# One GpSimd chain for both layer norms of a chunk, and a new order in the preparation of chunk 0, in a Mamba and MoE kernel

## The reference, cut to what matters

```python
# x is (8, 1024, 256); ED = 512 channels, N = 16 states, K = 4 taps
x = x + attn(_layernorm(x))        # a Mamba block
x = x + ffn(_layernorm(x))         # a shared expert and routed experts

# in attn:
xz = einsum('bld,ed->ble', x, in_proj_w); xp, z = halves of xz
xc = silu(causal depthwise conv of xp over 4 positions)
dBC = xc @ x_proj_w.T              # dt (64), Bm (16), Cm (16)
delta = softplus(dt @ dt_proj_w.T + dt_proj_b)
dA = exp(delta * A);  BX = delta * Bm * xc
hs = scan over positions of h = dA * h + BX      # per channel and state
y = sum over n of hs * Cm + D * xc
out = (y * silu(z)) @ out_proj_w.T

def _layernorm(x, eps=1e-05):
    m = mean(x); v = var(x)
    return (x - m) / sqrt(v + eps)
```

## Time and profile before

| | us |
|---|---|
| median of 3 runs (1570.89 to 1573.24) | 1572.64 |
| profiled execution, its own time | 1570.26 |
| its span in the trace | 1568.1 |
| mean granted TensorE clock | 0.993 |
| DVE busy | 1474.4 (94%), 1773 instructions |
| PE busy | 1448.2 (92%) |
| POOL busy | 1410.3 (90%), 1248 instructions |
| ACT busy | 1257.9 (80%) |
| DVE scans, L950 | 1165.5 (1024 of 1201 ns) |
| POOL products, L1238 | 1210.4 (512 of 2365 ns) |
| POOL u, L1256 | 81.7 (64 of 1276 ns) |
| POOL power, L1266 and L1277 | 16.2 and 15.1 (16 and 15 of about 1.01 us) |

### The profile page before, as it was taken

One profiled execution on the slowest core, in us unless ns is written; L12 is line 12 of the kernel. 1 busy time (PEld: TensorE's weight loads), 2 busy tenths in 40 slices (PEclk: granted clock), 3 DMA queues, 4 the chain that ended last, 5 costly groups with the idle time before them and its releaser, 6 DMA issues.

```text
span 1568.1 us, 39429 instructions
## 1 busy us (share of the span) xinstructions
PE 1448.2 (92%) x15188; PEld 1124.8 (72%) x15188; DVE 1474.4 (94%) x1773; ACT 1257.9 (80%) x2100; POOL 1410.3 (90%) x1248
## 2 busy tenths in 40 slices
PE   8889999999999999999999999999999999998887
PEld 5666777676776777777777776777777776776776
DVE  6999999999999999999999999999999999998885
ACT  7887887887888888887887888888887887787761
POOL 2899999999999999999999989999998999999993
PEclk9999999999999999999999999999999999999999
DMA  5103032040402204031040402204031030402201
GB/s 155 65 3 136 2 97 69 7 158 3 136 29 69 96 3 162 2 100 65 13 152 3 136 28 71 95 3 162 2 102 63 13 139 3 150 2 70 95 15 42
DMA packets 78514, 106.49 MB, mean 68 GB/s; under 512 B 42289, under 2 KB 67761, under 8 KB 70130
## 3 DMA queue, kind: packets, MB, share of 16 engines
q1 hardware_dynamic: 78322, 103.92, 20.7%
HBM read 86.10 MB, written 17.30 MB: 66 GB/s over the span
## 4 chain that ended last, share of the span: by engine, by line
DVE 31%; PE 20%; ACT 19%; issue 15%; POOL 10%; DMA 2%; SPq 1%; DVEq 1%; ACTq 0%; POOLq 0%
DVE hs L950 27%; PE BX L236 9%; ACT da L614 8%; POOL hs L1238 8%; PE Y L296 4%; PE Y L260 3%; DMA cb<-c_scratch 1%; ACT xc L681 1%; ACT x2n L751 1%; PE PB L346 1%; SPq L1367 1%; DVE st L962 1%; ACT xp L649 1%; ACT u L719 1%; DVE Y L981 1%
## 5 line engine op out<-in xcount | busy, mean ns | idle before, releaser
L1238 POOL TENSOR_TENSOR hs<-hs,cb 128x1024 f32<-128x1024 f32 x512 | 1210.4, 2365 | 67.2 <-DVE hs L950 45.2
L950 DVE TENSOR_TENSOR_SCAN hs<-da,BX 128x512 f32<-128x512 f32 x1024 | 1165.5, 1201 | 59.8 <-PE BX L236 50.5
L614 ACT ACTIVATE da<-delta,a_neg 128x511 f32<-128x511 f32 (+1 forms) x1024 | 663.6, 711 | 24.9 <-DVE hs L950 24.4
L260 PEld LDWEIGHTS Y<-ident,hs 128*128 128x128 f32 x4096 | 467.4, 141 | 92.9 <-issue 62.5
L260 PE MATMUL Y<-ident,hs 128*128 128x128 f32 x4096 | 514.0, 274 | 8.5 <-POOL hs L1238 8.5
L236 PE MATMUL BX<-bd,uT 32*128 32x128 f32 x8192 | 303.1, 285 | 96.6 <-DVE hs L950 91.4
L236 PEld LDWEIGHTS BX<-bd,uT 32*128 32x128 f32 x8192 | 253.7, 187 | 157.3 <-DVE hs L950 155.0
L296 PE MATMUL Y<-xnT,w_in 128*128 128x512 f32 x240 | 119.5, 621 | 0.9 <-ACT xnT L630 0.9
L649 ACT ACTIVATE xp<-Y 128x512 f32<-128x512 f32 x60 | 35.9, 598 | 101.2 <-PE Y L296 100.7
L321 PE MATMUL PA<-w_in,xnT 128*128 128x512 f32 x240 | 114.5, 599 | 0.0
L981 DVE SCALAR_TENSOR_TENSOR Y<-xp,w_conv,Y 128x512 f32<-128x512 f32 x120 | 88.9, 741 | 2.6 <-ACT Y L651 0.9
(11 more groups left out here) (186 smaller groups left out, 1496.9 us busy)
## 6 DMA issues: line engine op xcount, KB each, us to landing
cb<-c_scratch SPq DMA_DIRECT2D x64, 1024.0 KB, 4.8
x<-in_x SPq DMA_DIRECT2D x16, 512.0 KB, 4.0
x_scratch<-x2T SPq DMA_DIRECT2D x16, 512.0 KB, 6.6
...
c_scratch<-dbc SPq DMA_DIRECT2D x64, 8.0 KB, 1.5
```

The lines of the kernel that those rows point to most:

```text
L260: mm = e.matmul(Y[(G * c + g) % 2][:, t * P:(t + 1) * P], hs[:, k % HR, q, t * P:(t + 1) * P], ident[:, :], is_transpose=True, start=False ...
L614: e.activation(da[:, k % DR, q, h:], delta[:, g, h:], ACT.Exp, scale=a_neg[:, g, n:n + 1]).then_inc(s_da, 1)
L950: e.tensor_tensor_scan(hs[:, k % HR, q, :], da[:, k % DR, q, :], BX[:, :].rearrange("p (t n) -> p n t", n=RT)[:, n % RT, :], float(c % HV) ...
L1238: e.tensor_tensor(hs[:, k % HR, :, :], hs[:, k % HR, :, :], cb[:, Q * p:Q * p + Q, :], ALU.mult).then_inc(s_hc, 1)
```

## The change

1. Buffers `mv`, `ve`, `rstd`, `neg`, `shift` become 8 columns wide; the first norm has columns 0 to 3, the second 4 to 7. In chunks 1 to 12 (`BOTH`) POOL runs one chain over all 8 columns at step 21, where it ran one of 4 columns at step 21 and another of 4 at step 25. Chunk 0 has its one chain (of 4) at step 21 instead of 25; chunks 13 to 15 keep theirs. Who waited for the second norm's semaphore now waits for the joint one (`shifted2`).
2. In the preparation of chunk 0: the norm of chunk 1 moves on ACT from ahead of the first evacuations to behind the second SiLU. DVE evacuates `dbc` in place of ACT. DVE computes the first `u` in place of POOL. The z projections 3 and 2, their evacuations, the first `act_exp` (now in two parts) and the `act_skip` of group 0 are put in another order.
3. At step 3 of chunk 0, PE runs 8 matmuls of the identity into `PA` whose result nobody reads.

```diff
@@ tensor
             pe_dbc(e, 0, 1)
-            pe_z_first(e, 3, (0,))
             pe_dt(e, 0, 0)
             pe_bt(e, 0)
             pe_dt(e, 0, 1)
-            pe_z_first(e, 3, (1,))
-            pe_z_first(e, 2)
+            pe_z_first(e, 3)
             pe_ut(e, 0, 0)
+            pe_z_first(e, 2, (0,))
             e.wait_ge(s_d1_out, 1)
             pe_bx(e, 0)
             pe_trc(e, 1, 0)
             pe_trc(e, 1, 1)
+            pe_z_first(e, 2, (1,))
...
+                    if c == 0 and s == 3:
+                        e.wait_ge(s_pa_out, a_use["trc", 1, 1] + 1)
+                        for _ in range(8):
+                            e.matmul(PA[:, 0:P], ident[:, :], ident[:, :], start=True, stop=True)
@@ scalar
             act_trc(e, 0, 1)
-            act_norm(e, 1)
...
             act_silu_first(e, 1)
+            act_norm(e, 1)
             act_silu_first(e, 2)
             act_z_first(e, 0)
-            act_z_first(e, 1)
             act_silu_first(e, 3)
             e.preload_act_table_set(EXPS)
-            act_dbc(e, 0)
+            act_z_first(e, 1)
...
-            act_exp(e, 0)
+            act_exp(e, 0, (0,))
             act_ut(e, 0, 0)
+            act_exp(e, 0, (1,))
             act_z_first(e, 3)
-            act_z_first(e, 2)
             act_exp(e, 1)
             act_trc(e, 1, 0)
             act_trc(e, 1, 1)
-            act_skip(e, 0, 0)
+            act_z_first(e, 2)
             act_exp(e, 2)
@@ vector
             dve_aggr(e, 2)
+            e.wait_ge(s_pa, a_use["dbc", 0, 0] + 1)
+            e.tensor_copy(dbc[0:FX, :].rearrange("f (j q t) -> f q j t", j=J, q=RT),
+                          PA[0:FX, :].rearrange("f (q j t) -> f q j t", j=J, q=RT)).then_inc(s_pa_out, 1)
             dve_stats(e, 3, 0)
             dve_stats(e, 3, 1)
             dve_bd(e, 0)
             dve_delta(e, 0, 0)
+            e.wait_ge(s_pb_out, b_use["dt", 0, 0] + 1)
+            e.wait_ge(s_xc, 1)
+            e.tensor_tensor(u[:, 0, :].rearrange("p (j q t) -> p q j t", j=J, q=RT),
+                            delta[:, 0, :].rearrange("p (q j t) -> p q j t", j=J, q=RT),
+                            xc[:, 0, :].rearrange("p (q j t) -> p q j t", j=J, q=RT), ALU.mult).then_inc(s_u, 1)
@@ gpsimd
         def pool_rstd(e, c):
             e.wait_ge(s_mv, TB * (c + 1))
             e.wait_ge(s_xn, c)
+            n = TB
+            if BOTH[0] <= c - 3 <= BOTH[1]:
+                n = 2 * TB
+                e.wait_ge(s_mv2, TB * (c - 3))
+                e.wait_ge(s_xn2, c - 4)
+            e.tensor_tensor(ve_b[:, 0:n], mv_b[:, 0:n, 1], epsv[:, 0:n], ALU.add).then_inc(s_ve, 1)
...
-            pool_u(e, 0, 0)
+            e.wait_ge(s_u, 1)
             pool_u(e, 0, 1)
...
-                    if s == 21 and on(c - 1):
+                    if s == 21 and c > BOTH[1]:
                         pool_rstd2(e, c - 1)
...
-                    if s == 25 and on(c + 3):
+                    if s == 21 and on(c + 3):
                         pool_rstd(e, c + 3)
```

More of the change, by code:

```diff
@@ L98, in mamba_moe @@
         mask = sb("mask", [P, KT])
-        mhalf = sb("mhalf", [P, TB])
-        minus = sb("minus", [P, TB])
-        epsv = sb("epsv", [P, TB])
+        mhalf = sb("mhalf", [P, 2 * TB])
+        minus = sb("minus", [P, 2 * TB])
+        epsv = sb("epsv", [P, 2 * TB])
         halo0 = sb("halo0", [P, G, K - 1])
@@ L172, in released, with shifted2 @@
             return out, n + 1
+        BOTH = (1, NQ - 4)
+        def shifted2(c):
+            return (s_sh, c + 5) if c + 1 <= BOTH[1] else (s_sh2, c + 1 - BOTH[1])
         def conv_bank(v):
@@ L597, in tensor, with act_exp @@
             e.matmul(Y[0][0:1, 0:1], any_p[:, :], ones[:, :], start=True, stop=True).then_inc(s_any, 1)
-        def act_exp(e, k):
+        def act_exp(e, k, parts=range(2)):
             c, i = divmod(k, S)
@@ L611, in act_exp @@
                     e.activation(first[:, g, :], a_neg[:, g, :], ACT.Exp, scale=delta[:, g, 0:1]).then_inc(s_dec, 1)
-            for q in range(Q):
+            for q in parts:
                 n = Q * p + q
@@ L743, in act_norm2 @@
         def act_norm2(e, c):
-            e.wait_ge(s_sh2, c + 1)
+            e.wait_ge(*shifted2(c))
             for kk in range(2):
@@ L829, in scalar @@
                     if c == 0 and s == 0:
+                        act_skip(e, 0, 0)
                         act_exp(e, 3)
@@ L1007, in dve_aggr2 @@
             e.wait_ge(s_st2, TB * (c + 1))
-            e.wait_ge(s_sh2, c)
+            if c:
+                e.wait_ge(*shifted2(c - 1))
             for t in range(TB):
@@ L1262, in pool_rstd @@
             e.wait_ge(s_xn, c)
[L1263 to L1264 removed]
+            n = TB
[4 more added lines that the diff above has]
+            e.tensor_tensor(ve_b[:, 0:n], mv_b[:, 0:n, 1], epsv[:, 0:n], ALU.add).then_inc(s_ve, 1)
+            e.tensor_tensor(neg_b[:, 0:n], mv_b[:, 0:n, 0], minus[:, 0:n], ALU.mult).then_inc(s_neg, 1)
             e.wait_ge(s_ve, c + 1)
[L1266 removed]
+            e.tensor_tensor(rstd_b[:, 0:n], ve_b[:, 0:n], mhalf[:, 0:n], ALU.pow).then_inc(s_rs, 1)
             e.wait_ge(s_neg, c + 1)
             e.wait_ge(s_rs, c + 1)
[L1269 removed]
+            e.tensor_tensor(shift_b[:, 0:n], neg_b[:, 0:n], rstd_b[:, 0:n], ALU.mult).then_inc(s_sh, 1)
         def pool_rstd2(e, c):
@@ L1273, in pool_rstd2 @@
             e.wait_ge(s_xn2, c)
-            e.tensor_tensor(ve2[:, :], mv2[:, :, 1], epsv[:, :], ALU.add).then_inc(s_ve2, 1)
-            e.tensor_tensor(neg2[:, :], mv2[:, :, 0], minus[:, :], ALU.mult).then_inc(s_neg2, 1)
-            e.wait_ge(s_ve2, c + 1)
-            e.tensor_tensor(rstd2[:, :], ve2[:, :], mhalf[:, :], ALU.pow).then_inc(s_rs2, 1)
-            e.wait_ge(s_neg2, c + 1)
-            e.wait_ge(s_rs2, c + 1)
-            e.tensor_tensor(shift2[:, :], neg2[:, :], rstd2[:, :], ALU.mult).then_inc(s_sh2, 1)
+            n = c + 1 - BOTH[1]
+            e.tensor_tensor(ve2, mv2[:, :, 1], epsv[:, 0:TB], ALU.add).then_inc(s_ve2, 1)
+            e.tensor_tensor(neg2, mv2[:, :, 0], minus[:, 0:TB], ALU.mult).then_inc(s_neg2, 1)
+            e.wait_ge(s_ve2, n)
+            e.tensor_tensor(rstd2, ve2, mhalf[:, 0:TB], ALU.pow).then_inc(s_rs2, 1)
+            e.wait_ge(s_neg2, n)
+            e.wait_ge(s_rs2, n)
+            e.tensor_tensor(shift2, neg2, rstd2, ALU.mult).then_inc(s_sh2, 1)
         def pool_gap(e, c):
```

29 lines of the change are left out of this document (10 added, 19 removed).

## The result

The changed kernel takes 1566.78 us (median of 7 runs, 1565.71 to 1568.23), the kernel before on the same chip 1571.09 (7 runs, 1567.69 to 1573.24). The ratio is 0.9971, 95% interval 0.9962 to 0.9981: 4.3 us faster. The interval (3.0 to 6.0 us) is clear of no change and just reaches the 3.1 us that I had called the edge of what can be told. The time lies inside the forecast range of 1566.6 to 1572.4, 2.7 us under the forecast of 1569.5; the kind of result that I had held likeliest, within 0.2%, did not come. The profiled execution of after took 1566.57 us with a span of 1564.7; the forecast for it was 1567.2.

The account below looks back on a forecast made before the run. It took a ring to bound each pair: four scans read one set of BX banks, then 16 matmuls refill it. Gains of 2.1 + 0.46 + 0.5 = 3.1 us off 1572.64 gave 1569.5 us, range 1566.6 to 1572.4.

Parts of the forecast that it names:

- the edge of what can be told: Whole kernel: a measurement can tell about 0.2%, 3.1 us, from no change; the forecast gain lay on it.
- within 0.2%: Whole kernel: the outcome of a time not clearly faster or slower than before; chance 0.49.
- the term for TensorE's clock: Chunk 0, step 3: matmuls filling PE's idle gap keep the clock up, gaining 0.5 us (bounds 0 and 0.6).
- Chain at step 25 removed, step 21 wider: Even chunks 2 to 12: late pair gone, 3.1 us gained; new wait costs 1.0; net 2.1 us.
- Odd chunks untouched: Odd chunks: slack of 0.97 us swallows POOL's 0.64 us delay; they still last 93.7 us.
- Preparation up to the first scan: Chunk 0: earlier `dbc` evacuation and `u` on DVE start the first scan at 34.5 in place of 35.74.
- Behind it: Chunk 0 after the first scan: most is given back; taps start at 40.5 for 40.94, leaving 0.46 us.
- The eight matmuls: Chunk 0, step 3: they fill about 1.9 us of PE's gap at no cost, gaining 0.5 us (0 to 0.6).
- the early slow stretch: Chunk 0, 47.0 to 50.5 us: TensorE partly at its lower clock; BX took 1.63 us for 1.17.
- The second slow stretch: Chunk 0, at 118.67 us: another clock drop behind a shorter PE gap; counted 0, though it may go (0.9).
- The base: Whole kernel: the time before, 1572.64 us, a median of runs, from which the gain of 3.1 us was taken.
- how the numbers follow: Closing step turning forecast and rivals into chances: faster 0.46, slower 0.05, the rest 0.49.

## Why the prediction was right and wrong

The step that failed is the size of the term for TensorE's clock. The sum had 0.5 us for it, 0.6 at most, and 2.1 + 0.46 = 2.56 for the rest. The means of all runs show 1.3 us that go with the clock and 2.9 at equal clock, 4.1 together for 3.1. That put the result on the far side of the 3.1 us that I took for the edge. Term by term:

- **Chain at step 25 removed, step 21 wider: right.** Forecast 3.1 - 1.0 = 2.1; the traces give 6 times 0.33 = 2.0. The power on 8 columns took 1640 ns for 1.63 us, there are 12 of them, the new pair at step 25 took 6.00 to 6.03 for "about 6.0", and PE waited 1.04 us for 1.06. The run with the joint chain alone shows the same even chunks of 93.90, and the run with the new preparation and two chains has the old ones of 94.24. By the rule of the Trainium skill that the prediction weighed ("GPSIMD Engine Reference", "Elementwise — side-by-side cycle accounting"), 4 more columns would cost an estimated 9 ns, and the pair at step 25 would stay at 5.85; this trace doesn't agree, with 626 ns.
- **Odd chunks untouched: right**, 93.73. The reason that I gave for their greater slack, no `hlast` copy, is loose: POOL makes the carried column there instead, which lasts as long (0.20 us). But a step of POOL takes 2.48 us in chunk 3 of the kernel before (product at 388.06, next one at 390.54) and 2.57 in chunk 2 (294.25, 296.82).
- **Preparation up to the first scan: right.** 34.63 for 34.5, the copy of `dbc` on DVE 0.69 for 0.67. **Behind it: right.** Taps at 40.55 for 40.5; 0.39 us for 0.46. The cause, the z evacuation in front of the projection, is confirmed by the run that moves it: 0.75 us came back.
- **The eight matmuls: the mechanism right, the size wrong.** I took 0.5 us (bounds 0 and 0.6) from the one execution that I had. There the early slow stretch cost 0.50. In two of six executions it cost 1.7 to 1.8; the mean is 0.9. My upper bound of 0.6 was no bound but a second reading of one instance. I had also thought that the gain would stand in some runs only; the stretch was there in all six executions without the matmuls. The term's own run on the kernel before gives a mean of 0.5, with 0.7 of uncertainty, and so can't correct this.
- **The second slow stretch, counted at 0: right for the change**, though the first comparison of traces seems to say otherwise. It is gone in one profiled execution of the changed kernel and there in the other. That agrees with the Trainium skill, "TensorE: Matmul & The Clock Gate", section "What's actually happening", by which the monitor runs free of the kernel's start.
- **The base: also wrong.** I took the gain off the median of three runs, 1572.64. Over 113 runs the kernel before has a mean of 1571.4, and beside after 1571.09. 3.1 us off that is 1568.0, in place of 1569.5. Of the 2.7 us between forecast and result, 1.5 are this, and 1.2 the gain itself, 4.3 for 3.1.
- **The step "how the numbers follow":** with a sum of 3.1 on the edge of 3.1, I gave "within 0.2%" 0.49 and "faster" 0.46. The side was set by which of the rivals lay beyond the edge, and I had entered the throttle only as one that takes gain away. It was the term that could add.

What stays open: the parts seen in the traces are 2.0 (chains), 0.4 (start) and 0.9 (clock, as a mean), 3.3 us. The difference of the means is 4.1, with some 0.4 of uncertainty. At equal clock it is 2.9, which leaves 1.3 for the clock rather than 0.9.

The 181 runs of the seven kernels that have or lack each of the three parts can be fitted together, one number for each part. At equal clock the fit gives the joint chain 2.4 us, the preparation 0.5 and the matmuls nothing, each to 0.2. In the mean clock it gives the matmuls 0.8 thousandths, worth 0.7 us, the chain 0.5 and the preparation 0.4, each with 0.4 of uncertainty. So the matmuls pay through the clock alone, and whether the two others raise the clock at all can't be told. Against the rest stand the six runs of the changed kernel without the eight matmuls: their mean clock of 0.9938 is as high as that of the runs with them. Whether that is chance was not settled.
